# Two gate rows spread over the partitions by DMA from DRAM copies instead of by TensorE and ScalarE, with two orders on VectorE changed

## The reference

```
x = x + conv_block(ln_c(x))       # layer norm over channels; windows of 8x8 tokens, 4 heads, softmax with a
                                  # relative bias, values, output projection with bias
t = tokens(x)                     # (batch, 128*128, 64)
t = t + moe(ln_t(t))              # layer norm of every token, router to 8 experts, softmax, the best 2,
                                  # shares scaled to a sum of 1, each expert a 64x64 product with bias
```

## Time and profile before

| | |
|---|---|
| median of three runs | 1341.95 us (1341.09 to 1342.88) |
| the profiled execution, device time | 1341.82 us |
| its span | 1340.0 us |
| busy share | PE 92%, DVE 85%, POOL 69%, ACT 65% |
| mean granted TensorE clock | 0.975 of 2.4 GHz |
| DMA | 91.53 MB moved in all, 27.0% of 16 engines for SP's queue |

### The profile page before, as it was taken

How to read it: one execution, slowest core, us unless ns; L and a number is a source line. 1 busy time by engine, 2 the same in 40 slices (tenths; PEclk the granted TensorE clock), 3 DMA queues, 4 the chain that set the end, 5 groups by cost and what they waited for, 6 DMA issues and landing times.

```text
span 1340.0 us, 47446 instructions
## 1 busy us (share of the span) xinstructions
PE 1237.9 (92%) x19840; PEld 781.4 (58%) x19840; DVE 1138.4 (85%) x2436; ACT 875.7 (65%) x1615; POOL 918.0 (69%) x809
## 2 busy tenths in 40 slices
PE   4579999999999999999999999999999999999986
PEld 3456666656666665665566566566566665666542
DVE  5548998998898899899888889989888888888865
ACT  5357677667666767767666777776667666666632
POOL 6456777777666777777766777876866667666642
PEclk8579999999999999999999999999999999999988
DMA  7012332322223233232222323322222222222221
GB/s 199 1 34 60 90 90 67 90 58 53 58 66 75 67 90 90 67 75 58 54 64 58 90 73 84 90 67 59 58 67 51 60 66 59 64 55 59 59 66 40
DMA packets 95554, 91.53 MB, mean 68 GB/s; under 512 B 26797, under 2 KB 62253, under 8 KB 95342
## 3 DMA queue, kind: packets, MB, share of 16 engines
q1 hardware_dynamic: 95342, 88.49, 27.0%
HBM read 36.03 MB, written 17.83 MB: 40 GB/s over the span
## 4 chain that ended last, share of the span: by engine, by line
PE 50%; DVE 23%; ACT 10%; issue 8%; POOL 7%; DMA 1%; SPq 1%; POOLq 0%; DVEq 0%; ACTq 0%
PE bank_y L523 10%; PE bank_s L407 8%; PE bank_s L381 6%; DVE t_g L950 6%; PE bank_t L422 5%; PE bank_o L435 4%; DVE mx L842 4%; DVE x L864 4%; PE bank_p L450 3%; PE bank_e L479 3%; ACT k_m L644 3%; PE bank_g L512 2%; DVE o_t L855 2%; ACT prob_t L668 2%; PE bank_e L472 2%
## 5 line engine op out<-in xcount | busy, mean ns | idle before, releaser
L1069 POOL TENSOR_TENSOR prob<-prob,mx 128x512 f32<-128x512 f32 x256 | 261.7, 1044 | 88.5 <-DVE mx L842 87.8
L523 PE MATMUL bank_y<-t_g,w_exp 128*64 128x512 f32 x1024 | 279.2, 622 | 16.7 <-DVE t_g L950 12.5
L664 ACT ACTIVATE prob<-prob 128x512 f32<-128x512 f32 x256 | 160.7, 628 | 147.4 <-POOL prob L1069 145.7
L1091 POOL TENSOR_TENSOR t_g<-t_t,g_copy 128x512 f32<-128x512 f32 x128 | 165.4, 1292 | 125.5 <-ACT g_copy L696 125.2
L668 ACT ACTIVATE prob_t<-bank_t 128x512 f32<-128x512 f32 x256 | 152.4, 595 | 135.8 <-PE bank_t L422 135.7
L1081 POOL TENSOR_TENSOR ln<-ln,mhalf 128x8 f32<-128x8 f32 x64 | 105.1, 1642 | 158.1 <-DVE ln L878 158.1
L835 DVE TENSOR_TENSOR prob<-bank_s,rel 128x1024 f32<-128x1024 f32 x128 | 156.6, 1223 | 39.7 <-PE bank_s L407 35.1
L422 PEld LDWEIGHTS bank_t<-idn,prob 128*128 128x128 f32 x1024 | 111.1, 144 | 130.2 <-issue 105.4
L422 PE MATMUL bank_t<-idn,prob 128*128 128x128 f32 x1024 | 169.1, 288 | 12.7 <-ACT prob_t L668 10.6
L950 DVE TENSOR_TENSOR t_g<-t_t,bank_p 128x512 f32<-128x512 f32 x256 | 174.3, 681 | 7.3 <-PE bank_p L512 6.9
L407 PEld LDWEIGHTS bank_s<-k_m,q_t 32*64 32x64 f32 x4096 | 114.0, 135 | 72.2 <-issue 68.6
(11 more groups left out here) (114 smaller groups left out, 2400.3 us busy)
## 6 DMA issues: line engine op xcount, KB each, us to landing
t_t<-t_rout SPq DMA_DIRECT2D x256, 128.0 KB, 2.4
x_in<-in_x SPq DMA_DIRECT2D x68, 256.0 KB, 3.3
r_b<-recip_rows SPq DMA_DIRECT2D x64, 256.0 KB
out_y<-y_out SPq DMA_DIRECT2D x128, 128.0 KB, 2.5
r_in<-sum_b SPq DMA_DIRECT2D x64, 16.0 KB
recip_rows<-r_out SPq DMA_DIRECT2D x64, 16.0 KB, 1.4
gate_sel<-in_sel SPq DMA_DIRECT2D x1, 512.0 KB
rel<-in_relb SPq DMA_DIRECT2D x1, 256.0 KB
```

What stands on the lines that cost most here:

```text
L523: mm(B_Y[C * a:C * a + C, :], w_exp[:, pair, :], t_g[:, (2 * pair + a) % TG, :], start=False, stop=(pair == MIXES // 2 - 1), skip_group_ch ...
L664: A(prob[:, i], prob[:, i], ACT.Exp).then_inc(p_ready.sem, 1)
L1069: G.tensor_tensor(sc, sc, mx[:, i, :].unsqueeze(2).broadcast_to([P, 2 * HEADS, NTOK]), ALU.subtract).then_inc(s_shifted.sem, 1)
L1091: G.tensor_tensor(t_g[:, u % TG, :], t_t[:, p, u % 2, :], g_copy[:, n % 2, :], ALU.mult).then_inc(tg_pool.sem, 1)
```

## The change

Units 4 and 5 take the place of 2 and 6 on GpSimd. Their gates no longer go over PE's selecting matmul and ACT's copy: DVE leaves the gates of a strip in SBUF (`g_f`), PE transposes them once more, in f32 (128x64 to 64x128), ACT copies the result to `g_rows`, SP writes it four times to DRAM (`gate_rows`, four copies), and four further transfers read each row of it 16 times from each of the four copies into `g_copy`. On SP the writes stand between `cut_sums` and `spread_reciprocals`, the reads between `spread_rows` and `spread_tokens`. On POOL both gates stand behind `normalise_input`. On DVE the second `maxima` moves ahead of `total_squares` and `reciprocals`, and gate 7 moves ahead of `add_input`. On PE the selecting matmuls of units 4 and 5 go, and that of unit 7 moves ahead of `project_out`.

```diff
@@ -43,7 +43,7 @@
 BANK = 512
 EXPERTS = 8
 MIXES = EXPERTS
-ON_POOL = (2, 6)
+ON_POOL = (4, 5)
 ON_DVE = tuple(u for u in range(MIXES) if u not in ON_POOL)
 TG = 4
 ROWS = 8
@@ -221,13 +223,16 @@
         e_ready = sem("e_ready", 2)
         gt_done = sem("gt_done")
         gt_ready = sem("gt_ready")
-        gate_done = sem("gate_done", MIXES)
-        g_copied = sem("g_copied", len(ON_POOL))
+        rows_ready = sem("rows_ready")
+        rows_kept = sem("rows_kept", 16 * COPIES)
+        gate_done = sem("gate_done", len(ON_DVE))
+        g_spread = sem("g_spread", 64)
         tg_dve = sem("tg_dve", MIXES - len(ON_POOL), primed=1)
         tg_pool = sem("tg_pool", len(ON_POOL))
         y_done = sem("y_done", MIXES, primed=1)
         y_ready = sem("y_ready", primed=1)
 
+        gate_rows = nc.dram_tensor("gate_rows", [COPIES, 2, EXPERTS, 4, P], F32).ap()
         recip_rows = nc.dram_tensor("recip_rows", [2 * HEADS, BANK], F32).ap()
 
         consts = [(w_qkv, wqkv), (b_qkv, qkvb), (k_mask, kmask), (k_bias, kbias), (w_proj, wproj), (w_rout, wrout),
@@ -297,9 +302,32 @@
 
                 sp.wait_ge(recip_ready.sem, recip_ready.at(g, 1))
                 sp.dma_start(recip_rows.rearrange("a (c x) -> (a c) x", x=CHUNK), r_out[:, :]).then_inc(recip_kept.sem, 16)
+
+            def spread_rows(g):
+
                 sp.wait_ge(recip_kept.sem, recip_kept.at(g, 16))
                 sp.dma_start(r_b[:, :], recip_rows.unsqueeze(1).broadcast_to([2 * HEADS, DH, BANK])
                              ).then_inc(recip_spread.sem, 16)
+
+            def keep_gates(g):
+
+                sp.wait_ge(rows_ready.sem, rows_ready.at(g, 1))
+                if g:
+                    sp.wait_ge(g_spread.sem, g_spread.at(g))
+                for n in range(COPIES):
+                    sp.dma_start(gate_rows[n].rearrange("a e k t -> k a e t"), g_rows[:, :]).then_inc(rows_kept.sem, 16)
+
+            def spread_gates(g):
+
+                sp.wait_ge(rows_kept.sem, rows_kept.at(g, 16 * COPIES))
+                if g:
+                    sp.wait_ge(tg_pool.sem, tg_pool.at(g))
+                for n, u in enumerate(ON_POOL):
+                    first = u // 2 * 2
+                    for e in range(2):
+                        src = gate_rows[:, u % 2, first + e].rearrange("n k t -> n (k t)")
+                        sp.dma_start(g_copy[C * e:C * e + C, n, :], src.unsqueeze(1).broadcast_to([COPIES, C // COPIES, BANK])
+                                     ).then_inc(g_spread.sem, 16)
 
             def spread_tokens(g, p):
 
@@ -320,8 +348,13 @@
                 projecting, attending, outputting, routing_on, mixing = stages(on)
                 if outputting:
                     cut_sums(j - 1)
+                if mixing:
+                    keep_gates(j - 3)
                 if outputting:
                     spread_reciprocals(j - 1)
+                    spread_rows(j - 1)
+                if mixing:
+                    spread_gates(j - 3)
                 if routing_on:
                     if outputting:
                         sp.wait_ge(recip_spread.sem, recip_spread.at(j - 1, 16))
@@ -485,7 +518,8 @@
                 pe.sem_inc(passed, 1)
                 gt16 = B_G[:, :].bitcast(BF16)
                 for k in range(4):
-                    last = tr(gt16[:, k * P:(k + 1) * P], g3[:, k].rearrange("p a e -> p (a e)"), idn16[:, :])
+                    tr(gt16[:, k * P:(k + 1) * P], g3[:, k].rearrange("p a e -> p (a e)"), idn16[:, :])
+                last = tr(B_G[0:ROWS * EXPERTS, BANK // 2:BANK // 2 + P], g_f[:, :], idn[:, :])
                 last.then_inc(gt_done.sem, 1)
 
             def residual(g, p):
@@ -505,10 +539,8 @@
 
                 if u == 1:
                     pe.wait_ge(sum_copied.sem, sum_copied.at(min(g + 2, LAST) if isinstance(g, int) else g + 2, 1))
-                elif u and u - 2 in ON_POOL:
-                    pe.wait_ge(g_copied.sem, g_copied.at(g, ON_POOL.index(u - 2) + 1))
                 elif u:
-                    pe.wait_ge(tg_dve.sem, tg_dve.at(g, ON_DVE.index(u - 2) + 1))
+                    pe.wait_ge(tg_dve.sem, tg_dve.at(g, ON_DVE.index(u) - 1))
                 mm(B_GATE[u % 2][:, :], gate_sel16[:, u, :], g_t[:, :], start=True, stop=True).then_inc(gate_done.sem, 1)
 
             def experts(g, pair):
@@ -562,8 +594,6 @@
                     experts(j - 3, 0)
                 if attending:
                     turn_probs(j, 2, work)
-                if mixing:
-                    gates(j - 3, 4)
                 if projecting:
                     scores(j + 1, 1 - p, 0)
                 if work.take:
@@ -573,12 +603,10 @@
                 if attending:
                     turn_probs(j, 3, work)
                 if mixing:
-                    gates(j - 3, 5)
                     gates(j - 3, 6)
+                    gates(j - 3, 7)
                 if outputting:
                     project_out(j - 1)
-                if mixing:
-                    gates(j - 3, 7)
                 if projecting:
                     turn_values(j + 1, attending)
                 if mixing:
@@ -689,11 +717,8 @@
 
             def copy_turned_gates(g):
                 act.wait_ge(gt_done.sem, gt_done.at(g, 1))
+                A(g_rows[:, :], B_G[0:ROWS * EXPERTS, BANK // 2:BANK // 2 + P], ACT.Copy).then_inc(rows_ready.sem, 1)
                 A(g_t[:, :], B_G[:, :].bitcast(BF16)[:, 0:BANK], ACT.Copy).then_inc(gt_ready.sem, 1)
-
-            def copy_gates(g, u):
-                act.wait_ge(gate_done.sem, gate_done.at(g, u + 1))
-                A(g_copy[:, ON_POOL.index(u) % 2, :], B_G[:, :], ACT.Copy).then_inc(g_copied.sem, 1)
 
             def copy_result(g):
                 act.wait_ge(y_done.sem, y_done.at(g, MIXES))
@@ -724,8 +749,6 @@
                     copy_probs(j, 1)
                 if attending:
                     exps(j, 2)
-                if mixing:
-                    copy_gates(j - 3, 2)
                 if projecting:
                     copy_q(j + 1, 1 - p)
                 if attending:
@@ -738,8 +761,6 @@
                     take(work.batch, *work.take, 1, B_T[:, :])
                 if attending:
                     copy_probs(j, 3)
-                if mixing:
-                    copy_gates(j - 3, 6)
                 if work.take:
                     square_planes(work.batch, *work.take, 1)
                 if work.step == PLANES:
@@ -884,8 +905,9 @@
             def routing(g, first_step, last_step):
 
 
-                logits, lg, lead, hot, rest, gates = (
-                    B_E[:, n * ROUTE_AT:(n + 1) * ROUTE_AT].rearrange("p (r e) -> p r e", e=EXPERTS) for n in range(6))
+                logits, lg, lead, hot, rest = (
+                    B_E[:, n * ROUTE_AT:(n + 1) * ROUTE_AT].rearrange("p (r e) -> p r e", e=EXPERTS) for n in range(5))
+                gates = g_f[:, :].rearrange("p (r e) -> p r e", e=EXPERTS)
                 def thrice(v, n):
                     return v.unsqueeze(2).broadcast_to([P, 4, n, 2 * EXPERTS])
 
@@ -959,16 +981,16 @@
                     token_variance(j - 2)
                 if mixing:
                     routing(j - 3, 15, 19)
+                if attending:
+                    maxima(j, 1)
                 if work.step == SQUARES:
                     total_squares(work.batch)
+                if outputting:
+                    reciprocals(j - 1)
                 if work.step == PLANES:
                     total_planes(work.batch)
                 if work.step == SCALES:
                     turn_root(work.batch)
-                if outputting:
-                    reciprocals(j - 1)
-                if attending:
-                    maxima(j, 1)
                 if mixing:
                     gate(j - 3, 1 - p, 0)
                     gate(j - 3, 1 - p, 1)
@@ -977,21 +999,20 @@
                 if routing_on:
                     routing(j - 2, 0, 8)
                 if mixing:
+                    gate(j - 3, 1 - p, 2)
                     gate(j - 3, 1 - p, 3)
-                    gate(j - 3, 1 - p, 4)
                 if projecting:
                     bias(j + 1, 0)
                 if outputting:
                     normalise(j - 1)
                 if mixing:
-                    gate(j - 3, 1 - p, 5)
+                    gate(j - 3, 1 - p, 6)
                 if projecting:
                     maxima(j + 1, 0)
+                if mixing:
+                    gate(j - 3, 1 - p, 7)
                 if outputting:
                     add_input(j - 1, 1 - p)
-                if mixing:
-                    gate(j - 3, 1 - p, 7)
-                if outputting:
                     token_mean(j - 1, 1 - p)
 
             pipeline(dve, slot, first_sums, first_statistics, lambda batch: None)
@@ -1084,7 +1105,7 @@
 
             def gate(g, p, u):
                 n = ON_POOL.index(u)
-                pool.wait_ge(g_copied.sem, g_copied.at(g, n + 1))
+                pool.wait_ge(g_spread.sem, g_spread.at(g, 64))
```

(5 more changed lines are left out.)

7 lines of the change are left out of this document (5 added, 2 removed).

## The result

| | before | after |
|---|---|---|
| median | 1341.55 us (1341.09 to 1342.88, 4 runs) | 1866.11 us (1862.42 to 1878.11, 4 runs) |
| the profiled execution, device time | 1341.82 us | 1868.14 us |
| its span | 1340.0 us | 1866.3 us |
| mean granted TensorE clock | 0.975 | 0.858 |

The ratio is 1.392, with a 95% interval of 1.386 to 1.399. The forecast was 1700 us with a range of 1540 to 1850: the side and the mechanism came out as written, the size did not, and the result lies 16 us above the range.

The account below looks back on a forecast made before the run. Bound now by PE's chain in plain slots, DVE in take slots; after, by a closed loop over the transfers: 8.1 + 2.1 + 1.4 + 2.9 + 6.0 + 0.7 + 2.6 = 23.8 us, plus 1.4 for the clock, 25.2 a slot: 1700 us, range 1540 to 1850.

Parts of the forecast that it names:

- Step 5: The four reads of the gate rows: four engines, the same each time, move 64 packets each at 94 ns, 6.0 us.
- 4 to 6: From r_b's issue to GpSimd's gates: r_b's packets 2.9 us, the four reads 6.0, last packet to waiting engine 0.7.
- Step 3: On SP, from recip_rows' issue to r_b's issue: 1.41 us, up to 0.5 more if its packets queue behind the writes.
- Step 2: SP's issues of the four writes of the gate rows: 2.1 us, bounds 1.3 and 2.5.
- Step 1: From GpSimd's gates' end to the end of PE's transposes, with the new transpose and the copy of the rows: 8.1 us.
- Step 7: Two gates on GpSimd, one behind the other: 2 x 1.30 = 2.6 us.
- The clock: PE idles some 5 us a slot, so part of its work runs at 1.2 GHz: 1.4 us a slot, bounds nothing and 4.2.
- The case with the clock at its full level: Reads on four engines, PE's clock stays: loop of 23.8 us, 273 us more, 1615 us; chance 0.26.
- the likeliest case: Reads on four engines and PE's clock falls in part: slot of 25.2 us, 1700 us, own range 1630 to 1800; chance 0.45.
- spread over more engines: Reads of the gate rows use more than four engines, about 2.6 us: loop of 20.4 us, 1410 us; chance 0.12.
- hidden: The transfers' landing costs nothing, plain slots lose 0.1 us and take slots 0.17: 8 us less, 1334 us; chance 0.06.
- part c: DVE's new order: maxima ahead of reciprocals removes a 0.99 us wait, gate 0 then waits for its matmul; take slots 0.17 us shorter.

Follow-up runs that it names:

- no_landing: The changed kernel, all transfers made, but GpSimd multiplies by a constant tile and doesn't wait for them (gates of units 4 and 5 missing from the result); 1347.2 us.
- reads16: The changed kernel with the four reads running over 64 partitions first and the four copies second, same bytes; 1441.1 us.
- pitch: The changed kernel with the four DRAM copies 34 KB apart instead of 32 KB; 1840.3 us.
- tokens_later: The changed kernel with the four transfers of the tokens issued only after the gate rows have landed; 1803.0 us.
- pitch_tokens: The changed kernel with copies 34 KB apart and the tokens' transfers issued only after the gate rows have landed; 1742.3 us.
- pitch_tokens_filled: The changed kernel with copies 34 KB apart, the tokens' transfers issued after the gate rows have landed, and 20 filler matmuls on PE in each slot; 1643.4 us.
- filled: The changed kernel with 24 filler matmuls in PE's idle time of each slot, ahead of the transposes of the values; 1772.1 us.
- maxima_only: The kernel before with only DVE's second maxima moved ahead of the totals and reciprocals, gate 7 staying behind the addition; 1342.8 us.

## Why the prediction was wrong in size and right in its mechanism

- **What bounds the kernel, and the closed loop**: right. GpSimd waits 543.7 us for `g_copy`, ACT and PE wait for GpSimd as written, and taking the wait away (no_landing) gives back all but 6 us.
- **Step 5, four engines**: the count was right (16 small packets for four reads, 64 in reads16). The pace was the mis-sized term. The 94 ns a packet came from `r_b`, whose neighbours in time are other rows of one small tensor and which had its engines to itself. The new reads start slowly from rows 32 KB apart and have the tokens' packets beside them: `r_b`'s issue to the gates took 0.73 + 10.51 = 11.2 us, not 9.6. The experiments split the 1.6: pitch gives 0.8 back and tokens_later 1.3, together 2.1. The steps' 9.6 held for the kernel with both gone (9.15 in pitch_tokens, 9.37 in pitch_tokens_filled). I had bounded the pace at 88 to 103 ns (5.6 and 6.6 us over 64) from rows of this one transfer. It was the bound that failed: no row showed four engines with other work beside them, and the text should have said that it had none. The pace itself, with nothing else moving, was even a little better than reckoned, 83 to 84 ns.
- **Step 3**: `recip_rows` to `r_b` 1.76 for 1.4; the 0.5 for its packets queueing behind the writes stood in the text as a possibility and not in the sum. **Step 2**: 2.30 for 2.1, inside its bounds. **Step 1**: 7.87 with the full clock, for 8.1. **Step 7**: 2.48 for 2.6.
- **The clock**: 1.8 us a slot for 1.4 by part A (9.69 against 7.87 in filled), 1.5 by the whole time; inside the bounds either way.
- **The sum**: 27.5 instead of 25.2 is +1.6 for the reads, +0.4 for step 3, +0.2 for step 2, +0.4 for the clock, and -0.2 and -0.1 for steps 1 and 7. The case with the clock at its full level was forecast at 1615 us with a loop of 23.8; pitch_tokens_filled has parts that sum to 23.8, slots of 24.1 and 1643 us. That both come to 23.8 is in part luck: steps 2 and 3 were 0.6 too small together there too, and steps 1, 4 to 6 and 7 were 0.5 too large.
- **The range**: each of the pace, the issues and the clock came out on the long side. 1875 us stood among the cases with a chance of 0.11, but for another reason (the clock low for most of the loop), and the range was cut at 1850, through it. The long bounds of the likeliest case add up to 26 + 4.2 = 30 us a slot (the bounds that the steps name come to 25.3 and not 26, which changes little), and 1850 stands for only 27.6: the long side had been given too little, with three terms of which no row showed the value itself.
- **The rival "spread over more engines"**, 1410 us: not what happened, but its price was about right. With sixteen engines it is 1441 us and a slot of 20.9 against the 20.4 given.
- **The rival "hidden"**, 1334 us: the nearest run, no_landing, is 1347. Its first half held for the typical plain slot (0.18 shorter in the one read above, 0.1 in the median of all, for the 0.1 given), part c for take slots was wrong (0.38 longer for 0.17 shorter). The matmul of gate 0 is not done 0.2 us before DVE asks for it once DVE asks earlier: it moves with the slot. maxima_only shows that wait for wait is what this order changes. What beyond it lengthens the take slots of no_landing is open: DVE's longer wait for bank G, 0.35 us a slot with the gate's 0.33 in it, has the right size, but no run takes it away.

## What to carry to other kernels

A transfer's pattern decided here on how many DMA engines it ran, and for a small broadcast on the path that was worth more than the number of copies: put an extent that 16 divides first, before thinking about copies (here 425 us by one line, and the four copies then brought nothing). Price a transfer by rows in which the same engines are as loaded as they will be; where no such row is there, widen the bound on the long side. When one engine's wait goes into a closed loop, add up the loop and not the busy shares, and add what the idle time does to the clock of the engine that idles.

## What the runs showed of the hardware

- Reading four rows at a time that lie 32 KB apart began slower than 34 KB apart: 25 packets of 2 KB a us against 50 in the first 1.5 us, then 50 in both (tokens_later and pitch_tokens), and 0.8 us of 10.5 by the distance alone. I had not expected any dependence on it.
- Four engines with nothing else moving took 83 to 84 ns for a packet of 2 KB.
- Sixteen engines reading one and the same 2 KB row 64 times were hardly slower than with four copies of it (5.51 and 5.35 us).
- Transfers issued later on the same queue slowed earlier ones: 10.5 us fell to 9.2 when the tokens' four were issued afterwards.
- Four transfers issued one behind the other mostly cost SP 2.2 to 2.5 us, 0.55 to 0.63 each. Some runs of four took longer, 3.52 and, for the tokens' in one slot of after, 5.38 us; why is open.
- TensorE's granted clock went to 1.2 GHz behind a stretch with 1.50 us of work in 6.40, and in the slot before was back at 2.4 after 3.7 us of unbroken work; it cost 1.5 to 1.8 us a slot.
